# A fused attention and expert block on eight cores: QKV matmuls of a core's own tokens moved in between the layer-norm tiles of the neighbour's tokens, and the output transposes cut in halves

## The reference, cut to what matters

```python
xn = _layernorm(x, axis=-1)
x = x + _L0_attn_ref(xn, Wqkv, bqkv, Wout, bout) + _L0_ffn_ref(xn, gate_weight, gate_up_proj, down_proj, layer_alpha)
# attention
qkv = x @ Wqkv + bqkv
q, k, v = jnp.split(qkv, [D, D + KV], axis=-1)
...
scores = jnp.einsum('bqhd,bkhd->bhqk', q, k) / HD
prob = jax.nn.softmax(scores, axis=-1)
out = jnp.einsum('bhqk,bkhd->bqhd', prob, v).reshape(b, s, D)
return out @ Wout + bout
# experts: routing on softmax(x @ gate_weight.T), then for each of the 32
gu = x @ w_gu.T
g, u = jnp.split(gu, 2, axis=-1)
h = jax.nn.silu(g) * u
acc = acc + h @ w_d.T * c_e[:, None]
```

## Time and profile before

| What | us |
|---|---|
| median of three runs | 5498.86 |
| the three runs | 5497.65, 5498.86, 6399.97 |
| profiled execution, its own time | 5498.15 |
| its span on the slowest core (core 0) | 5496.4 |
| spans of the eight cores | 5486.5 to 5496.4 |
| mean granted TensorE clock of the cores, 1 is full | 0.955 to 0.962 |

### The profile page before, as it was taken

The page is one execution under the profiler, slowest core; times in us unless marked ns, Lnnn a source line. Parts: engine busy times, 40 slices in busy tenths (PEclk is TensorE's granted clock), DMA queues, the critical chain, the costliest instruction groups (busy, mean ns, idle before and its releaser), DMA issues.

```text
span 5496.4 us, 62961 instructions; the slowest of 8 cores (5486.5 to 5496.4 us)
## 1 busy us (share of the span) xinstructions
PE 4948.5 (90%) x23551; PEld 2342.3 (43%) x24008; DVE 1720.9 (31%) x2480; ACT 747.3 (14%) x1045; POOL 259.5 (5%) x493
## 2 busy tenths in 40 slices
PE   3589666688999999999999999999999999999995
PEld 2434443343444444444444444444444444444443
DVE  3300666611322223222333332232222223233333
ACT  4311555521000000000000000000000000000000
POOL 0000000000000000000000000000000000000000
PEclk8589999999999999999999999999999999999997
DMA  5231000035444444444433434444444444443333
GB/s 171 77 62 31 1 1 1 1 58 101 76 74 73 73 73 74 74 75 74 73 70 70 81 70 76 75 73 74 75 74 74 73 73 75 75 74 70 69 64 124
DMA packets 79878, 378.29 MB, mean 69 GB/s; under 512 B 9696, under 2 KB 10848, under 8 KB 65248
## 3 DMA queue, kind: packets, MB, share of 16 engines
q0 software_dynamic: 70416, 323.03, 33.2%
q1 hardware_dynamic: 9168, 51.21, 2.8%
HBM read 688.80 MB, written 8.39 MB: 127 GB/s over the span
## 4 chain that ended last, share of the span: by engine, by line
PE 86%; ACT 5%; DVE 3%; DMA 3%; issue 2%; ACTq 0%; DVEq 0%; SPq 0%; POOLq 0%
PE ps_a L821 49%; PE ps_d L757 24%; ACT p_exp L577 4%; PE ps_a L490 4%; PE ps_a L562 2%; PE ps_a L679 2%; PE ps_d L629 2%; PE ps_b L789 1%; PE ps_b L394 1%; DMA x_re<-x_own 1%; DMA wgubuf<-gu 1%; PE ps_b L353 1%; PE ps_d L378 0%; DMA xtile<-x_own 0%; DVE ffn_acc L767 0%
## 5 line engine op out<-in xcount | busy, mean ns | idle before, releaser
L821 PE MATMUL ps_a<-xn_own,wgubuf 128*128 128x512 bf16 x12044 | 2692.3, 384 | 26.6 <-DMA wgubuf<-gu 12.5
L821 PEld LDWEIGHTS ps_a<-xn_own,wgubuf 128*128 128x128 bf16 x12288 | 1211.6, 99 | 1517.9 <-issue 104.6
L757 PE MATMUL ps_d<-hstash,wdbuf 128*128 128x512 bf16 x6016 | 1330.5, 379 | 11.1 <-DVE ffn_acc L767 0.9
L844 DVE TENSOR_TENSOR sg_sb<-ps_a,sg_sb 128x512 f32<-128x512 f32 x384 | 265.7, 692 | 2409.2 <-PE ps_a L821 2409.2
L757 PEld LDWEIGHTS ps_d<-hstash,wdbuf 128*128 128x128 bf16 x6144 | 595.9, 97 | 741.5 <-issue 182.1
L767 DVE TENSOR_TENSOR ffn_acc<-ffn_acc,ps_d 128x512 f32<-128x512 f32 x1024 | 704.2, 688 | 606.2 <-PE ps_d L757 602.5
L834 ACT ACTIVATE sg_sb<-ps_a 128x512 f32<-128x512 f32 x384 | 229.3, 597 | 2261.5 <-PE ps_a L821 2261.5
L60 POOL DMA_DIRECT2D wgubuf<-gu x384 | 203.5, 530 | 2603.6 <-PE ps_a L821 2554.7
L562 PE MATMUL ps_a<-k_sb,q_sb 128*128 128x512 bf16 x470 | 133.2, 405 | 207.4 <-ACT p_exp L577 131.6
L849 DVE TENSOR_TENSOR hstash<-sg_sb,c_rep 128x512 bf16<-128x512 f32 x384 | 266.0, 693 | 39.9
L799 ACT ACTIVATE c_rep<-ps_b 128x512 f32<-128x512 f32 x64 | 38.2, 597 | 1534.3 <-PE ps_b L789 1485.3
(11 more groups left out here) (98 smaller groups left out, 1104.0 us busy)
## 6 DMA issues: line engine op xcount, KB each, us to landing
wgubuf<-gu POOLq DMA_DIRECT2D x384, 512.0 KB, 6.2
wdbuf<-down POOLq DMA_DIRECT2D x64, 1536.0 KB, 10.8
xtile<-x_own SPq DMA_DIRECT2D x16, 1024.0 KB, 5.7
xtile<-x_nbr SPq DMA_DIRECT2D x16, 1024.0 KB, 5.6
wjbuf<-wqkv POOLq DMA_DIRECT2D x24, 512.0 KB, 5.1
woutbuf<-wout POOLq DMA_DIRECT2D x16, 512.0 KB, 5.1
x_re<-x_own SPq DMA_DIRECT2D x8, 1024.0 KB, 6.9
o<-out_sb SPq DMA_DIRECT2D x8, 1024.0 KB, 4.9
```

The source lines that it names most:

```text
L757: ins = e_.matmul(ps_d[:, slot * 512:(slot + 1) * 512], wdbuf[gh % 3][:, (dc % 8) * 768 + icc * 128: (dc % 8) * 768 + icc * 128 + 128], hs ...
L821: ins = e_.matmul(ps_a[:, bank * 512:(bank + 1) * 512], wgubuf[bufi][:, dc * 128:(dc + 1) * 128], xn_own[:, dc * TOWN + tb * 512: dc * TOW ...
L844: ev_h1[(e, ip, tb)] = B.op("vector", lambda e_, tb=tb: e_.tensor_tensor(sg_sb[:, tb * 512:(tb + 1) * 512], ps_a[:, (2 + tb) * 512:(3 + tb ...
```

## The change

Three edits.

**Own-token QKV work moves into the layer-norm loop.** The QKV stage becomes functions that are called in two places. 20 chunks (all 16 of queries, and the 4 of keys for the own tokens alone) are emitted inside the loop, after the body of tile t = 7 to 14: three chunks after each of t = 7 to 11, two after t = 12 and 13, one after t = 14. That is 40 groups. After the routing and its barrier, `emit_qkv_nbr` does the rest: keys for the neighbour's tokens (chunks 16 to 19 with two groups each) and values (chunks 20 to 23 with four), 24 groups. The weights of chunks 16 to 19 are loaded twice, so there are 28 weight DMAs instead of 24. The first two weight DMAs are issued early: chunk 0 after the statistics, chunk 1 after the f32 transposes of tile 6.

**Buffers move.** `la_all` to `fb_all` of the routing go from the bytes that `q_sb` uses to bytes that `vt_sb` uses later, and the two `wjbuf` go to a free place behind all buffers and to the place of `xnf0`, which is dead after tile 6.

**The output stage is cut in halves.** PE transposes 8 blocks instead of 16 for each DVE addition, which has 128x1024 instead of 128x2048; half `hf` of a block uses one half of `ps_a` and waits for the addition two halves earlier.

```diff
-    wjbuf = [sb(f"wjbuf{i}", [128, DC * 128], BF16, DYN + i * 4096) for i in range(2)]
+    wjbuf = [sb("wjbuf0", [128, DC * 128], BF16, 204800),
+             sb("wjbuf1", [128, DC * 128], BF16, 40960)]
...
+    def emit_wj_dma(jc, use, nbr=False):
+        key = (jc, nbr)
+        prev = wj_order[wj_order.index(key) - 2] if wj_order.index(key) >= 2 else None
+        if prev is not None:
+            B.wait("gpsimd", "st", ev_jchunk_done[prev])
+        ev_wj[key] = B.dma("gpsimd", wjbuf[use][:],
+                           dwqkv[jc].rearrange("p a b -> p (a b)"), f"swj{use}")
...
+    wj_order = [(jc, False) for jc in range(20)] + [(jc, True) for jc in range(16, 24)]
+
+    def emit_qkv_own_chunk(jcs):
+        for jc in jcs:
+            if wj_order.index((jc, False)) >= 2:
+                emit_wj_dma(jc, wj_order.index((jc, False)) % 2, nbr=False)
+            for tblk in (0, 1):
+                emit_qkv_group(jc, tblk, nbr=False)
+
+    def emit_qkv_nbr():
+        B.wait("tensor", "sv", ev_tpb_evac[15][1])
+        for jc in range(16, 24):
+            if wj_order.index((jc, True)) >= 2:
+                emit_wj_dma(jc, wj_order.index((jc, True)) % 2, nbr=True)
+            g = jc - 16 if jc < 20 else jc - 20
+            tblks = (2, 3) if jc < 20 else (0, 1, 2, 3)
+            for tblk in tblks:
+                emit_qkv_group(jc, tblk, nbr=True)
...
+        if t == 7:
+            B.wait("gpsimd", "ss", ev_sq1[15])
+            emit_wj_dma(0, 0, nbr=False)
+            B.wait("gpsimd", "st", ev_tpf[6][1])
+            emit_wj_dma(1, 1, nbr=False)
+            B.wait("tensor", "ss", ev_sq1[15])
+            B.wait("tensor", "sv", ev_tpb_evac[7][1])
+            emit_qkv_own_chunk([0, 1, 2])
+        elif t == 8:
+            emit_qkv_own_chunk([3, 4, 5])
...
+        elif t == 14:
+            emit_qkv_own_chunk([19])
...
-        if tc >= 1:
-            B.wait("tensor", "sv", ev_osb[tc - 1])
...
+        for hf in range(2):
+            gen = tc * 2 + hf
+            bs = (gen % 2) * 1024
+            if (gen - 2) in ev_add:
+                B.wait("tensor", "sv", ev_add[gen - 2])
...
+            ev_add[gen] = B.op("vector", lambda e, tc=tc, hf=hf, bs=bs: e.tensor_tensor(
+                out_sb[tc % 2][:, hf * 1024:(hf + 1) * 1024],
+                ps_a[:, bs:bs + 1024],
+                x_re[tc % 2][:, hf * 1024:(hf + 1) * 1024], ALU.add), "sv")
+        ev_osb[tc] = ev_add[tc * 2 + 1]
```

More of the change, by code:

```diff
@@ L316, in build_program, with xn_mv @@
     B.wait("scalar", "sv", ev_ln)
+    ev_wj = {}
+    ev_jchunk_done = {}
+    qkv_psum_free = [None, None, None, None]
+    qkv_rr = [0]
+    vst_evt = [None, None]
+    ev_qkv_ev = {}
+    ev_vt_evac_last = [None]
+    def xn_mv(dc, tblk):
+        srct = xn_own if tblk < 2 else xn_nbr
+        off = dc * TOWN + (tblk % 2) * 512
+        return srct[:, off:off + 512]
+    def emit_wj_dma(jc, use, nbr=False):
[5 more added lines that the diff above has]
+                           dwqkv[jc].rearrange("p a b -> p (a b)"), f"swj{use}")
@@ new lines, in emit_qkv_group, with qkv_mm @@
+    def emit_qkv_group(jc, tblk, nbr):
+        key = (jc, nbr)
+        use = wj_order.index(key) % 2
+        bank = qkv_rr[0] % 4
+        qkv_rr[0] += 1
+        B.wait("tensor", f"swj{use}", ev_wj[key])
+        B.wait("tensor", "ss", qkv_psum_free[bank])
+        def qkv_mm(e, jc=jc, tblk=tblk, bank=bank, use=use):
+            for dc in range(DC):
+                ins = e.matmul(ps_a[:, bank * 512:(bank + 1) * 512],
+                               wjbuf[use][:, dc * 128:(dc + 1) * 128],
+                               xn_mv(dc, tblk),
+                               start=(dc == 0), stop=(dc == DC - 1))
+            return ins
+        ev_mm = B.op("tensor", qkv_mm, "st")
+        ev_jchunk_done[key] = ev_mm
+        g = jc - 20 if jc >= 20 else (jc - 16 if jc >= 16 else None)
+        if jc < 16:
+            ddst = q_sb[:, jc * TOWN + tblk * 512: jc * TOWN + tblk * 512 + 512]
+        elif jc < 20:
+            ddst = k_sb[:, g * S + tblk * 512: g * S + tblk * 512 + 512]
+        else:
+            ddst = vstage[g % 2][:, tblk * 512: tblk * 512 + 512]
+        B.wait("scalar", "st", ev_mm)
+        if jc >= 20 and tblk == 0 and g >= 2:
+            B.wait("scalar", "st", vst_evt[g % 2])
+        if jc < 16:
+            ev_qkv_ev[(jc, tblk)] = B.op(
+                "scalar", lambda e, d=ddst, bank=bank, jc=jc:
+                e.activation(d, ps_a[:, bank * 512:(bank + 1) * 512],
+                             AF.Identity, bias=bqkv128[:, jc:jc + 1],
+                             scale=1.0 / HD), "ss")
+        else:
+            ev_qkv_ev[(jc, tblk)] = B.op(
+                "scalar", lambda e, d=ddst, bank=bank, jc=jc:
+                e.activation(d, ps_a[:, bank * 512:(bank + 1) * 512],
+                             AF.Identity, bias=bqkv_sb[:, jc:jc + 1]), "ss")
+        qkv_psum_free[bank] = ev_qkv_ev[(jc, tblk)]
@@ L460, in build_program @@
     B.barrier()
[L462 to L539, removed]
@@ L541, in build_program @@
+    emit_qkv_nbr()
     B.barrier()
```

74 lines of the change are left out of this document (52 added, 22 removed).

## The result

Some executions of every kernel here, of the one before too, are slowed on four or all eight cores by a lower clock and are left out, and of one kernel (`c3_all_three`) only the four cores that were not slowed can be read.

| | before | changed |
|---|---|---|
| profiled execution | 5498.15 us | 5532.66 us |
| others | 5497.65 to 5506.77 | 5528.5, 5528.7, 5563.6 |
| ratio | | 1.0074, 95% interval 1.0045 to 1.0103 |

A forecast was written before the change was run, and what follows sets the result against it. Experts' matmuls, 73% of the span, stay untouched; at most 32.6 us winnable. Added: tiles 47.2, copy 0.9, clock 14.0, output 2.0, together 64.1; less 32.6, net +31.5 on 5498.15: 5530 us, range 5510 to 5554.

The forecast's parts named there:

- What can be won: Layer-norm loop, neighbour's tiles: at most 32.6 us, 0.6% of the time; the routing's 46.68 us not in reach.
- ACT's lead is lost: Loop: six evacuations stand ahead of each normalization, so PE idles 3.2 us after each set's last group.
- A tile costs 5.9 us: Neighbour's tiles in the loop: idle PE plus two batches with DVE's copy between, 5.4 to 6.3 us; eight tiles 47.2 us.
- The clock: Loop: PE's clock falls at every pause, 1.75 us for each of eight sets, 14.0 us; bounds 2.0 and 20 us.
- Rival 1: Loop: the clock holds through the pauses, clock cost 2.0 us; +15.5, 5514 us; chance 0.17.
- the V pauses: Old QKV stage, V transposes: pauses of about 3 us; one cost 1.52 us of clock, one at 504 spared it.
- Groups and weights: Loop and QKV: 40 groups of 3.45 us, 138 us wherever they stand; weight loads in the loop hidden by about 1.2 us.
- rival 4: Loop: weights late because xtile loads are in flight with them; up to 21 us more, 5551 us; chance 0.10.
- The sum: Whole kernel: 64.1 us added, 32.6 removed, net +31.5, giving 5530 us, 0.6% slower.
- The output stage: Output stage: halved additions take 0.25 us more per block, 2.0 us over eight; PE running ahead wins nothing.
- Rival 2, the overlap works,: Loop: normalization is off PE's path, a pause is two batches, 2.23 us; -9.9, 5488 us; chance 0.06.

The follow-up runs named there:

- c3_all_three: Against the changed kernel: normalization first, two ps_b halves, 7 own chunks beside the routing, unhalved output stage with loads ahead of stores; spans 5395 to 5407 us (cores 0-3).
- c1: Changed kernel with all 20 own chunks moved from the loop to beside the routing, and the old output stage; 5450.9 to 5459.0 us, ratio 0.9916 to before.
- a1: Changed kernel with ACT's normalization of tile t+1 emitted ahead of the groups that follow tile t; 5492.0 to 5500.8 us, one of 5549.7, ratio 1.0012 to before.
- a3: Changed kernel with the output stage of the kernel before (one addition of 2048 columns per block); one execution, 5538.4 us.

## Why the prediction was right, point by point

- *What can be won.* The routing's 46.68 us were out of reach of the change: 46.80 after. Right, and c1 shows that they were the place to go.
- *ACT's lead is lost.* The wait that ends PE's pause was 3.28 us (said: 3.2), released by `xnbf` eight times out of eight. a1 took that order away and this wait went to nothing.
- *A tile costs 5.9 us.* This was too low. The pauses on core 0 are 6.14, 6.23, 6.14, 6.54, 6.15, 5.71, 6.14 and 6.32, 49.4 in all, for 47.2. The clock fell sooner than I assumed: the second batch ran at the low one in all eight, the first in two, and a set is picked up 0.2 us late.
- *The clock.* Said: it falls at every pause, 14.0 us. This was too high. The first group of a set was evacuated 5.19, 4.63, 4.30, 5.87, 4.78, 4.42, 4.71 and 5.90 us after its first matmul, where 3.56 is the full clock on that core; with two second groups 0.3 over, 11.9 us. It did fall at every one: on the eight cores, 64 pauses, it fell 2.1 to 5.4 us after the last group each time. The Trainium skill, TensorE: Matmul & The Clock Gate, section "HAM oscillation — how this bites in real kernels", has this pattern, each burst paying the start; the traces agree, with 1.5 us per set. Rival 1, the clock that holds, is what a1's pauses of 2.3 us do. The evidence for it was read too thin: the V pauses of about 3 us were counted as one fall and one escape, and the earlier trace rows has a second escape, the 3.77 us behind the transposes at 487.06. On all eight cores of the kernel before the clock fell at 6 of 24 of them.
- *Groups and weights.* 3.45 us a group wherever it stands at the full clock, and no wait for weights in the loop: right, rival 4 fell. What is behind the loop up to the first exp became 138 us shorter (167.3 in, 29.3 left over), as said.
- *The sum.* Gate to last copy: 200.1 predicted (138 + 47.2 + 14.0 + 0.9), 199.8 measured. Gate to exp +29.5 predicted, +29.3 measured. The mechanism is right, but that it came to 0.3 us is luck: the pauses were 2.2 us too low and the clock 2.1 too high.
- *The output stage.* +2.0 predicted for additions that are 0.25 us longer per block; 2.1 measured, on every core. The profile has +4.1; the other 2 are loads that landed late in that execution, and loads as late are seen without halves too (a3). That the halves win nothing was right as long as the loads are late.
- *Rival 2, the overlap works,* was priced at 5488 us and given 0.06 as the kernel stands. With the order mended it is real: a1 is at 5492.0 to 5500.8 us, and from the gate to the exp 13.7 us under the kernel before, where the rival's terms without the output stage come to 11.9.

What stays open: why some loads of `x_re` take 2 us longer than others, how much of the halves' 1.3 us behind early loads is more than chance, and why a pause of about 3 us sometimes costs the clock and mostly doesn't.

## What to carry to other kernels

Work that is put into a waiting engine's gaps is put into the streams of its helpers too. Before moving it, write down for each engine what now stands ahead of the instruction that the next phase waits for; here six evacuations ahead of one normalization turned an overlap into eight pauses, and moving the normalization forward was worth 43 us of the 363 between gate and attention, 27 of idle time and 14 of clock in the loop of core 0. And look for the place where the engine has nothing at all to do, the 47 us of routing, rather than for the one where its share is low because of short waits.
